# Mixture-of-experts decoder layer on one core: two adding transfers of 8 KB pieces in the last group of experts instead of four of 4 KB

## What is computed

```python
    def _L0_ffn_ref(hidden_states, gate_w, e_bias, w1, w2, shared_up_w, shared_down_w):
        E = 64
        K = 6
...
        CAP = 128
...
        idx, wts = _router(x, gate_w, e_bias)
        shared = _relu2(x @ shared_up_w.T) @ shared_down_w.T
        routed = _moe(x, idx, wts.astype(x.dtype), w1, w2)
        return (shared + routed).reshape(orig)
...
    x = x + _L0_ffn_ref(_layernorm(x, axis=-1), L0_ffn_gate_w, L0_ffn_e_bias, L0_ffn_w1, L0_ffn_w2, L0_ffn_shared_up_w, L0_ffn_shared_down_w)
```

## Time and profile before

| | us |
|---|---|
| median of 3 runs (983.96 to 991.77) | 989.09 |
| profiled execution | 995.12 |
| its span | 993.3 |
| TensorE (PE) busy | 901.2 |
| VectorE (DVE) busy | 551.3 |
| POOL busy | 462.4 |
| ScalarE (ACT) busy | 232.5 |

### The profile page before, as it was taken

The page is one execution under the profiler, slowest core; times in us unless marked ns, Lnnn a source line. Parts: engine busy times, 40 slices in busy tenths (PEclk is TensorE's granted clock), DMA queues, the critical chain, the costliest instruction groups (busy, mean ns, idle before and its releaser), DMA issues. The chain is left out here.

```text
span 993.3 us, 14608 instructions
## 1 busy us (share of the span) xinstructions
PE 901.2 (91%) x4947; PEld 626.9 (63%) x4947; DVE 551.3 (56%) x1143; ACT 232.5 (23%) x716; POOL 462.4 (47%) x512
## 2 busy tenths in 40 slices
PE   4899999998899999989999999998989799979980
PEld 3566666664677777766444586867666667666650
DVE  4688889767688888887888323222223122222220
ACT  1465646462400100122110021211111111111110
POOL 1545252634487888620272343444435244544422
PEclk9979999999999999999999999999999899999995
DMA  7300000020533333032007567898889789889863
GB/s 290 112 1 2 1 2 1 2 75 1 208 106 99 97 93 92 1 147 108 1 1 275 178 195 243 261 267 217 262 242 267 216 236 278 252 228 260 258 149 53
DMA packets 44142, 143.41 MB, mean 144 GB/s; under 512 B 7296, under 2 KB 11648, under 8 KB 35136
## 3 DMA queue, kind: packets, MB, share of 16 engines
q1 hardware_dynamic: 27424, 98.56, 27.0%
q0 software_dynamic: 14912, 37.76, 19.2%
q10 hardware_dynamic: 1760, 6.49, 1.7%
HBM read 114.36 MB, written 28.43 MB: 144 GB/s over the span
## 5 line engine op out<-in xcount | busy, mean ns | idle before, releaser
L1359 PE MATMUL ps<-arena 128*128 128x128 f32 (+4 forms) x2112 | 512.8, 401 | 10.1 <-DVE arena L812 5.7
L1359 PEld LDWEIGHTS ps<-arena 128*128 128x128 f32 x2112 | 337.9, 192 | 148.6 <-issue 103.7
L600 POOL DMA_INDIRECT out<-arena,scatter_rows x64 | 101.3, 1582 | 221.6 <-DMA out<-arena,scatter_rows 154.5
L1293 DVE TENSOR_TENSOR arena<-arena 128x256 f32<-128x256 f32 x64 | 27.3, 427 | 229.4 <-ACT arena L797 219.4
L1359 PE MATMUL ps<-features_T,arena 128*128 (+2 forms) x640 | 116.0, 338 | 0.0
L1359 PEld LDWEIGHTS ps<-features_T,arena 128*128 128x128 f32 x640 | 84.7, 188 | 37.3 <-issue 37.3
L650 ACT ACTIVATE arena<-ps 128x512 f32<-128x512 f32 (+1 forms) x137 | 78.5, 591 | 120.7 <-PE ps L1640 49.0
L472 POOL TENSOR_TENSOR arena<-arena 128x512 f32<-128x512 f32 x48 | 49.3, 1056 | 89.0 <-DVE arena L832 89.0
L797 ACT ACTIVATE arena<-ps 128x256 f32<-128x256 f32 x64 | 24.5, 383 | 264.6 <-PE ps L1359 245.4
L589 POOL DMA_INDIRECT arena<-token_rows,gather_rows x64 | 66.2, 1035 | 38.2 <-DVE gather_rows L1286 27.1
L660 ACT ACTIVATE arena<-arena 128x128 f32<-128x128 f32 x192 | 74.0, 389 | 16.7 <-DVE arena L820 16.7
(11 more groups left out here) (178 smaller groups left out, 1088.7 us busy)
## 6 DMA issues: line engine op xcount, KB each, us to landing
arena<-wexp SPq DMA_DIRECT2D x48, 1024.0 KB
residual<-wexp SPq DMA_DIRECT2D x16, 1024.0 KB
arena<-toeplitz_rows SPq DMA_DIRECT2D x32, 256.0 KB, 3.1
arena<-ctxE SPq DMA_DIRECT2D x32, 192.0 KB, 3.2
residual<-x SPq DMA_DIRECT2D x4, 1024.0 KB, 5.4
token_rows<-arena SPq DMA_DIRECT2D x16, 256.0 KB, 2.3
arena<-suT ACTq DMA_DIRECT2D x1, 2048.0 KB, 7.7
arena<-sdT ACTq DMA_DIRECT2D x1, 2048.0 KB, 12.6
```

The lines of the kernel that those rows point to most:

```text
L600: pool.indirect_dma_start(out, bass.IndirectOffsetOnAxis(ap=idxs[:, s % NY:s % NY + 1], axis=0), ysb[:, s % NY, :], None, compute_op=ALU.a ...
L1359: ins = TE.matmul(out_ap, lhsT, rhs, start=(n == 0), stop=(n == len(pairs) - 1))
```

## The change

The upper tokens are dealt to the tiles in another order: half `g` of group `j` takes tokens 4t + j (t from 0 to 127) of the g-th block of 512, so TensorE reads them from `x3T` at a step of four elements, before at a step of two. After four groups the four tiles of one `g` make 128 pieces of four rows, 8 KB each. DVE copies each tile to the residual's lower half, which is free once it is stored (a wait on `out_written`). All eight tiles stay there, and the last group sends them in two adding transfers: those of g = 0 ahead of the scatter of that group's expert 10 (expert 58 of all), those of g = 1 ahead of the last (expert 63). The other groups have no tile link. The chain has 66 links: 16, 16, 16 and 18. The indices of both transfers are written once, ahead of the loop.

```diff
-        LINKS = GROUP + 1
+        TILE_LINKS = (GROUP - 6, GROUP - 1)
...
-        ytile = carve([2, D], at=0)
-        htile = carve([SHD // P, P])
+        htile = carve([SHD // P, P], at=1024)
+        tiles_out = X[:, 0:NT // 2, :].rearrange("p (g j) d -> p g j d", g=2)
...
-            def scatter_tiles(j):
-                pool.wait_ge(tile_ready, j + 2)
-                pool.wait_ge(added, j * (16 * LINKS) + 16 * (GROUP - 1))
+            def scatter_tiles(g, before):
+                pool.wait_ge(tile_ready, g + 1)
+                pool.wait_ge(added, before)
                 pool.sem_inc(scatter_landed, 1)
-                pool.indirect_dma_start(out.rearrange("(r g) d -> r (g d)", g=2),
-                                        bass.IndirectOffsetOnAxis(ap=idxt[:, 0:1], axis=0),
-                                        ytile.rearrange("p g d -> p (g d)"), None, compute_op=ALU.add)\
+                pool.indirect_dma_start(out.rearrange("(r j) d -> r (j d)", j=4),
+                                        bass.IndirectOffsetOnAxis(ap=idxt[:, g:g + 1], axis=0),
+                                        tiles_out[:, g, :, :].rearrange("p j d -> p (j d)"), None, compute_op=ALU.add)\
                     .then_inc(added, 16)
...
             def group(j, more):
+                tiles = 0
                 for r in range(GROUP):
                     n = r + 1
-                    if n == GROUP - 1:
-                        scatter_tiles(j)
+                    if not more and n in TILE_LINKS:
+                        scatter_tiles(tiles, j * (16 * GROUP) + 16 * (n + tiles))
+                        tiles += 1
                     if n < GROUP:
-                        scatter(n % UE, j * 2 + n // UE, j * (16 * LINKS) + 16 * (n if n < GROUP - 1 else n + 1))
+                        scatter(n % UE, j * 2 + n // UE, j * (16 * GROUP) + 16 * (n + tiles))
...
-                        if g == 0:
-                            dve.wait_ge(scatter_landed, j * LINKS + NY)
-                        V.tensor_copy(ytile[:, g, :], ps[:, 7, :]).then_inc(empt[7], 1)
-                        if g == 1:
-                            V.tensor_copy(idxt[:], tile_rows[:, ds(j, 1)])
+                        dve.wait_ge(out_written, 16 * 3)
+                        V.tensor_copy(tiles_out[:, g, ds(j, 1), :].rearrange("p j d -> p (j d)"), ps[:, 7, :])\
+                         .then_inc(empt[7], 1)
+                        if end:
                             V.drain().then_inc(tile_ready, 1)
...
-                rows = [x3T[:, c, T // 2:T].rearrange("p (j t g) -> p j t g", t=P, g=2)[:, ds(j, 1), :, g]
-                        .rearrange("p j t -> p (j t)") for c in range(DC)]
+                rows = [x3T[:, c, T // 2:T].rearrange("p (g t j) -> p g t j", t=P, j=4)[:, g, :, ds(j, 1)]
+                        .rearrange("p t j -> p (t j)") for c in range(DC)]
```

More of the change, by code:

```diff
@@ L98, in program @@
         idxs = sb("scatter_rows", [P, 4], u32)
-        idxt = sb("tile_scatter_rows", [P, 1], u32)
-        tile_rows = sb("tile_rows", [P, NT // 4])
+        idxt = sb("tile_scatter_rows", [P, 2], u32)
+        tile_rows = sb("tile_rows", [P, 2])
         begun_mark = sb("begun_mark", [P, 1])
@@ L371, in _ @@
             load(dcol[:], "skip", small_loaded)
-            for s in (*empt, *conv_used, *conv_filled, *y_filled, *y_ready, hsq_ready, tile_ready):
+            for s in (*empt, *conv_used, *conv_filled, *y_filled, *y_ready, hsq_ready):
                 sp.sem_inc(s, 1)
@@ L431, in _ @@
                     load_expert(s, i)
-            sp.wait_ge(added, 16 * (E + NT // 4))
+            sp.wait_ge(added, 16 * (E + len(TILE_LINKS)))
         @block.gpsimd
@@ L442, in _ @@
             G.memset(kpad[:, 0:P], 0.0)
-            G.iota(tile_rows[:], [[P, NT // 4]], base=T // 4, channel_multiplier=1, allow_small_or_imprecise_dtypes=True)
+            G.iota(tile_rows[:], [[P, 2]], base=T // 8, channel_multiplier=1, allow_small_or_imprecise_dtypes=True)
             G.drain()
@@ L624, in group @@
             def group(j, more):
+                tiles = 0
                 for r in range(GROUP):
                     n = r + 1
-                    if n == GROUP - 1:
-                        scatter_tiles(j)
+                    if not more and n in TILE_LINKS:
+                        scatter_tiles(tiles, j * (16 * GROUP) + 16 * (n + tiles))
+                        tiles += 1
                     if n < GROUP:
-                        scatter(n % UE, j * 2 + n // UE, j * (16 * LINKS) + 16 * (n if n < GROUP - 1 else n + 1))
+                        scatter(n % UE, j * 2 + n // UE, j * (16 * GROUP) + 16 * (n + tiles))
                     elif more:
-                        scatter(0, j * 2 + 2, j * (16 * LINKS) + 16 * LINKS)
+                        scatter(0, j * 2 + 2, j * (16 * GROUP) + 16 * GROUP)
                     if more or r < UE:
@@ L1286, in _ @@
             V.tensor_copy(idxg[:], idxU[:, 0:UE]).then_inc(idx_ready, 1)
+            V.tensor_copy(idxt[:], tile_rows[:])
             for j in range(1, 3):
@@ L1294, in hidden_squared, with experts @@
                  .then_inc(hsq_ready, 1)
-            def experts(j, g, more):
+            def experts(j, g, more, end=False):
                 i = j * 2 + g
@@ L1306, in experts @@
                         dve.wait_ge(full[7], FE.filled(("tile_dn",), i))
-                        if g == 0:
-                            dve.wait_ge(scatter_landed, j * LINKS + NY)
-                        V.tensor_copy(ytile[:, g, :], ps[:, 7, :]).then_inc(empt[7], 1)
-                        if g == 1:
-                            V.tensor_copy(idxt[:], tile_rows[:, ds(j, 1)])
+                        dve.wait_ge(out_written, 16 * 3)
+                        V.tensor_copy(tiles_out[:, g, ds(j, 1), :].rearrange("p j d -> p (j d)"), ps[:, 7, :])\
+                         .then_inc(empt[7], 1)
+                        if end:
                             V.drain().then_inc(tile_ready, 1)
                     dve.wait_ge(y_filled[s], i + 2)
-                    dve.wait_ge(scatter_landed, j * LINKS + (r + 1 if r < NY - 1 else r + 2))
+                    dve.wait_ge(scatter_landed, j * GROUP + (r + 2 + (1 if end and r - NY >= TILE_LINKS[0] else 0)))
                     dve.wait_ge(xg_loaded[s], i * 16 + 16)
@@ L1333, in _ @@
                 experts(j, 1, True)
-            experts(E // GROUP - 1, 0, True)
-            experts(E // GROUP - 1, 1, False)
+            experts(E // GROUP - 1, 0, True, True)
+            experts(E // GROUP - 1, 1, False, True)
         @block.tensor
```

## The result

The changed kernel takes 1015.66 us in the median of 6 runs (1013.32 to 1017.5), the kernel before 987.23 beside it. The ratio is 1.029, with a 95% interval of 1.025 to 1.033. The prediction said 982, with 976 to 993 as its range. The time is outside, on the other side, and what happened is the first rival: TensorE took the bound.

What follows compares the result with a forecast made beforehand. The chain of adding transfers was taken as the bound. -20.8 - 6.67 + 2 x 9.15 + 2 = -7.2 us took the profiled 995.12 to 988; the profiled run's 6 us above the median made it 982, range 976 to 993.

Steps and rivals of the forecast that it cites:

- the first rival: TensorE takes the bound if the step of four doubles the up parts: median near 1004 us; chance 0.15.
- The bound of before: Experts' stage: the chain of adding transfers sets the time; finished rows wait 13, 19 and 19 us for it.
- The 14 us in hand: TensorE's slack in each group of 16 experts: 92 us of work against the chain's 106.
- Below 9 us a group it is hidden: Extra TensorE time in the up parts below 9 us a group was to be covered by its slack.
- the one on TensorE's up parts: Upper tokens read at a step of four: bounds nothing to 14.4 us a group; taken as nothing.
- The rival's arithmetic: TensorE as bound: group 106.4 us, expert 63's rows at 994, span 1008, median near 1004; chance 0.15.
- Tile links removed: First three groups lose their tile links from POOL's chain: 20.8 us off, leaving 98.8 us for 16 links.
- 2 given back: Short scatter links behind tile links in the first three groups are lost: 0.7 us a group, 2 in all.
- Large links: Last group: two links of 8 KB pieces, 9.15 us each, replace one of 6.67; bounds 7.9 to 11.6.
- The sum: Whole kernel: all terms together give -7.2 us, for a forecast of 982 us.
- The DMA rival: DMA engines at their 0.86 share take the saving back: groups of 101.6 us, total 989; chance 0.17.

Runs made afterwards that it cites:

- e2: The changed kernel with TensorE's up parts reading the upper tokens at a step of two again, both large links kept; 981.69 us, ratio 0.994.
- e4: e2 with both large links left out, so the shared expert's output for the upper tokens is never added; 959.5 us, ratio 0.969.
- e5: The changed kernel with a group's four up parts read contiguous, at a step of three, in pairs eight apart, and at a step of eight; 981.91 us, one execution.
- e6: The changed kernel without the first of its two large links, so four upper tiles are never added; 1010.98 us, ratio 1.022.
- e7: e2 with the shared expert's up-part weights, the stationary operand, read at a step of four elements; 1014.41 us in one execution.

## Why the prediction was wrong, point by point

- **The bound of before** was read rightly. e2 and e4 show it from both sides: with the step of two, links added and removed count.
- **The 14 us in hand** are those against 106 us with 17 links. They don't outlast the change: without the tile link the chain's groups take 95.4 and 97.4 us (98.8 in the prediction's sum) against TensorE's 92 (91.3 by starts: 3.60 is how long a down part is busy, its step is 3.43 in e2's trace), and e5, with 5.6 us more, has used up TensorE's idle time. "Below 9 us a group it is hidden" looked at expert 63's rows alone and is not shown; the runs show it for 5.6.
- **The failed step is the one on TensorE's up parts**: "A step of four is not in the trace; the bounds are nothing and the doubling ... I take nothing." The doubling is what came: 3.71 us for each up part, 14.8 a group against the 14.4 of the bound. The reason given against it, that an fp32 instruction "asks little of the memory", was an argument without a row. The earlier trace rows showed a step of two as free, and with two elements in each 16-byte line that row can't speak for a step of four. Of the bounds taken for the terms of the sum, it was the only one that changed the sign of the result, and 0.15 was too low for it. What the runs showed in its place: TensorE set the pace of every group (106.2 us), and POOL waited 88.6 us for rows made from its output.
- **The rival's arithmetic** held where it counted. It put expert 63's rows at 994 (993.9), the group at 106.4 (106.2). The span it gave was 1008, and 1013.8 was measured. The last large link started at 998.21, not 993: it waits for the landing of expert 62's scatter, and the chain was behind by the first large link. e6 gives that 3 us. The other 2 or so are expert 62's link itself: even in e6, where that scatter starts as soon as its rows are there, the large link starts 3.1 us after DVE has copied the last tile (988.31 to 991.38), and the rival allowed 0.9. The other part of the gap to the median, 1004 against 1016, is the 6 us by which the profiled execution of before lay above its median; that of the changed kernel lies on it (1015.6).
- **Tile links removed**: -20.8 with 2 given back. In e2 groups of 16 links took 95.4 and 97.4 us, not 98.8: nothing was given back that shows in these groups. In the changed kernel the term gave nothing, since TensorE sets the pace there.
- **Large links**: 9.15 forecast; 9.42, 9.34, 9.48 and 9.14 measured. Each doubling of the bytes added about twice what the one before had (5.59, 6.67, then 9.1 to 9.5), so from 2 to 8 KB pieces the adding transfer's time goes with bytes. By the slope of the Trainium skill (DMA: Bandwidth & Descriptors, Anatomy of one DMA), 1.2 us for 512 KB, set on the 6.67 of before, it would have been an estimated 7.9: these rows don't agree with that slope.
- **The sum**, -7.2 us or 0.993, is what the change is worth without the step: e2 has 0.994 and 981.69 for the 982 that was forecast. That it is this close is in part luck: its two halves were off by 6.2 and 3.4 us in e2's trace, in opposite directions, and executions differ by about 1%.
- **The DMA rival** (0.17) fell by e2's share of 0.91 and its groups of 95.4 and 97.4 us, where it had 101.6.

## What to carry to other kernels

When a layout is changed so that a transfer's pieces get longer, look at who reads the same data on the other side. TensorE's fp32 reads at a step were priced here by the 16-byte lines they touched, so a free step of two said nothing of a step of four. An idle time in hand is measured against the pace of before, and a change that speeds up the bound shrinks it. Give an unknown whose bound alone would move the bottleneck a chance of its own size, not that of an afterthought, or measure it first. And put the cost of a reorder on an idle engine: eight copies on ACT gave the transfers their order here, hidden in a gap of 49 us that ACT had in the kernel before.

## What was not expected of the hardware

- fp32 matmul instructions of 128 columns, which take 113 ns each, still slow down to 229 to 233 ns when each column's element lies in another 16-byte line, and weight loads slow down at a step of four too (188 to 328 ns in the mean, e2 and e7).
- ACT copied 512 elements from SBUF at a step of four in 1.05 us; its copies of 512 from PSUM, contiguous, take 0.60. Whether the step or the source makes the difference wasn't tried.
- In kernels that are bound by the chain too, a few scatter links take much longer than the usual 5.3 to 6.6 us. In e2 three of those between 600 and 940 us take 9.5 to 9.7 (one is 647.2 to 656.7, of which POOL waited 6.5 us for the landing, where 2.2 to 4 is usual). What makes these is open. At 3 to 4 us each they could make part of the 1% by which executions of one kernel differ, but no run was made to show that.
